# Keys laid out without padding in the attention of a hybrid kernel: two heads to 32 rows

## The chip, the cores and the metric

The kernel runs on one core of a Trainium2 chip. The metric is the device time in microseconds of one execution; with several runs, their median. TensorE (PE in the profile) multiplies matrices and transposes, VectorE (DVE) and ScalarE (ACT) work elementwise and take results out of PSUM, GpSimd (POOL) does small work, SyncE (SP) issues the DMAs.

## The reference, cut to what matters

One layer of a hybrid model runs over x of 4 x 1024 x 256, float32: a state-space block with a sequential scan over time, a mixture of 8 experts, an attention block with an MLP, and the same mixture again. The change touches the attention:

```
q, k, v = (einsum('bsd,dhm->bshm', x, w) for w in (wq, wk, wv))     # 16 heads of 16
phi_q, phi_k = relu(q) + 0.001, relu(k) + 0.001
kv  = cumsum(einsum('bshm,bshd->bshmd', phi_k, v), axis=1)
num = einsum('bshm,bshmd->bshd', phi_q, kv)
den = einsum('bshm,bshm->bsh', phi_q, cumsum(phi_k, axis=1))
attn_out = einsum('bshm,hmd->bsd', num / den[..., None], wo)
```

It is causal linear attention: within a chunk of 64 positions it is computed by scores and a mask, and what lies before the chunk comes in through running sums of phi_k v^T.

## The kernel before

A first part (`front_part`) normalises x, projects it, convolves, and writes the operands of the scan to DRAM; meanwhile SyncE loads the weights of the second part (L265). The second part (`main_part`) goes through the 1024 positions in 16 chunks of 64 positions by 4 batches, 256 tokens each (`TOK`), as two tiles of 128. Its loop is a software pipeline by hand: step i runs the scan of chunk i, the middle of chunk i-1 (gating, first mixture, attention) and the late part of chunk i-2 (MLP, second mixture). `step(1, 0, None)` has no late part and `step(None, 15, 14)` has no scan; so the attention runs 16 times, 14 of them in passes with all three parts.

Every engine's order is written out by hand, and engines meet only at semaphores.

- *Scan, VectorE.* 32 pairs of time steps to a chunk. One pair (`scan_pair`) is four multiplications (L1390) and four saturating additions (L1400), each on half the columns; a pair depends on the one before. After every fourth pair a small cblk product (L1375) follows.
- *Scan, TensorE.* `scan(1)` issues the inputs of the next pair, n+1 (`scan_inputs`, L974), which wait on `stepped` until VectorE has finished pair n-1, since they overwrite its bank; every fourth time the outputs of eight steps follow (`scan_output`, L989).
- *Attention, TensorE.* `features(w, j, made)` projects half of the key or query columns into bank `NB[j]`: 4 matmuls, each of which appears as two instructions in the trace (L1132). Values: L1290, into bank TB. `turn_k(tile)` (L1138) transposes the keys of one tile into TB, and ScalarE copies them to `ktok` (`copy_k`, L888). `scores` (L1149) has 128 small matmuls with 32 rows each; `from_states` (L1159), `from_chunk` (L1169) and `new_states` (L1180) follow.
- *Attention, VectorE.* `feature` (L1497) takes relu and adds epsilon from the bank into `kT` or `qT`, once for each half; `mask` (L1504) multiplies the scores.
- *Second mixture, beside it.* `late_first(e)` (L1055) and `late_second(e)` (L1068) are the layers of expert e of chunk i-2, `relu` (L879) lies between them on ScalarE, and `add_late(e)` (L1487) adds the result on VectorE. The scores wait for the fifth of these sums (`acc_done[1]`, `TILES * 5`), since they write its bank.

A head has 16 features, but the matmuls of the scores take rows in blocks of 32. So in the kernel before, wq and wk are padded: every head has 32 columns, of which the last 16 are zero, and 16 heads fill 4 groups of 128 rows (`GROUPS`), in q and in k.

## Time and profile before

| | |
|---|---|
| median of 3 runs | 2313.54 us (2308.51 to 2318.12) |
| the profiled execution | 2318.22 us, its span 2316.4 us |
| mean granted TensorE clock | 0.923 of full |
| TensorE (PE) busy | 1998.9 us, 86%, 18400 instructions |
| VectorE (DVE) busy | 1715.8 us, 74%, 6417 instructions |
| ScalarE (ACT) busy | 516.6 us, 22% |
| GpSimd (POOL) busy | 260.9 us, 11% |

A row of the timeline gives the start, the time from the first to the last end of the instructions that it merges, the engine, the line of the kernel, what is written and read, and the count; the bracket has the engine's idle time before it and who ended it. PE is the matmul itself and PEld the load of its weights; the ends of matmuls are modelled, and they are pipelined, so rows can overlap. In the chain that ended last, each piece is the time that the step added to the chain. Granted clock 1.00 is TensorE at 2.4 GHz and 0.50 at 1.2 GHz; a value between is a mean over a stretch.

### The profile page before, as it was taken

The page shows a single profiled execution, that of the slowest core. Times are in us where ns is not written, and L with a number is a line of the kernel's source. Part 1 is how long each engine was busy: PE and PEld are TensorE (multiplying, and loading weights), DVE is VectorE, ACT ScalarE, POOL GpSimd, SP SyncE. Part 2 cuts the span into 40 slices and gives each one's busy share as a digit, 9 for nine tenths or more (in the row PEclk, how much of TensorE's full clock was granted, in tenths as well). Part 3 has the DMA queues.
Part 4 walks back from the last instruction along what each step waited for, and adds up shares of the span by engine and source line. Part 5 has one row for each costly group of instructions (what it writes and reads, how often), then busy time and mean ns, then how long its engine had stood idle before and what let it go on. Part 6 is the DMA issues. An engine that isn't in the chain of part 4 may idle for free.

```text
span 2316.4 us, 59053 instructions
## 1 busy us (share of the span) xinstructions
PE 1998.9 (86%) x18400; PEld 1666.0 (72%) x18400; DVE 1715.8 (74%) x6417; ACT 516.6 (22%) x1078; POOL 260.9 (11%) x337
## 2 busy tenths in 40 slices
PE   7855788989898988989898989889898989899897
PEld 4432566878787877868787778778687877688786
DVE  4539777878787888778787878887887878787542
ACT  3330112122222222121212222221222122221221
POOL 0012002010101110010101110010101011100110
PEclk9865788999999999989998989999999999998998
DMA  7741100000000001000100101010001001010000
GB/s 254 222 119 31 30 12 22 14 25 12 19 23 12 25 12 30 12 26 14 27 12 15 26 11 26 12 30 12 25 13 29 12 12 30 11 27 7 6 2 10
DMA packets 100872, 73.51 MB, mean 32 GB/s; under 512 B 64488, under 2 KB 94448, under 8 KB 99568
## 3 DMA queue, kind: packets, MB, share of 16 engines
q1 hardware_dynamic: 100592, 69.91, 10.7%
q8 instruction: 160, 2.62, 0.5%
q14 instruction: 120, 0.98, 0.1%
HBM read 46.26 MB, written 23.59 MB: 30 GB/s over the span
## 4 chain that ended last, share of the span: by engine, by line
PE 54%; DVE 19%; issue 9%; SPq 7%; POOL 1%; DMA 1%; DVEq 1%; ACT 1%; POOLq 0%
PE bank L1068 17%; PE bank L1055 12%; DVE decayed_state L1390 6%; PE bank L1132 5%; DVE state L1400 4%; PE bank L974 4%; PE bank L989 3%; PE bank L1169 3%; PE bank L1010 2%; SPq L706 2%; SPq L724 1%; SPq L715 1%; PE bank L1202 1%; SPq L723 1%; SPq L722 1%
## 5 line engine op out<-in xcount | busy, mean ns | idle before, releaser
L1390 DVE TENSOR_TENSOR decayed_state<-state,decay 128x128 f32<-128x128 f32 x2048 | 567.7, 318 | 12.5 <-issue 8.7
L1400 DVE CUSTOM_DVE_ANT_0 state<-decayed_state,bank 128x128 f32<-128x128 f32 x2048 | 501.2, 285 | 61.5 <-PE bank L974 29.8
L1068 PE MATMUL bank<-f_w_sb,hs_whole 128*128 128x256 f32 x2048 | 510.1, 393 | 4.1 <-ACT hs_whole L879 4.1
L1068 PEld LDWEIGHTS bank<-f_w_sb,hs_whole 128*128 128x128 f32 x2048 | 382.5, 196 | 72.2 <-ACT hs_whole L879 21.7
L879 ACT ACTIVATE hs_whole<-bank,f_b_sb 128x256 f32<-128x256 f32 x512 | 214.7, 470 | 938.7 <-PE bank L1055 938.7
L974 PE MATMUL bank<-xrows,brows 128*128 128x256 f32 x1024 | 258.2, 345 | 87.1 <-DVE state L1400 53.4
L974 PEld LDWEIGHTS bank<-xrows,brows 128*128 128x128 f32 x1024 | 180.2, 212 | 130.4 <-issue 68.1
L1487 DVE SCALAR_TENSOR_TENSOR x<-bank,comb,x 128x256 f32<-128x256 f32 x256 | 111.8, 478 | 131.4 <-PE bank L1068 130.9
L989 PE MATMUL bank<-state,cblk 128*32 128x256 f32 x2048 | 156.4, 428 | 54.7 <-DVE state L1400 49.3
L1487 DVE SCALAR_TENSOR_TENSOR res<-bank,comb,res 128x256 f32<-128x256 f32 x256 | 112.1, 479 | 122.5 <-PE bank L1068 121.1
L801 POOL TENSOR_TENSOR m_ve<-m_mv,m_eps 128x2 f32<-128x2 f32 x96 | 19.2, 200 | 1539.8 <-DVE m_mv L1424 1539.8
L1055 PE MATMUL bank<-late_fT_parts,f_w_hi 128*128 128x256 f32 x1024 | 184.9, 304 | 0.0
L1055 PE MATMUL bank<-fT_parts,f_w_hi 128*128 128x256 f32 x1024 | 176.3, 299 | 0.0
L1055 PEld LDWEIGHTS bank<-late_fT_parts,f_w_hi 128*128 128x128 f32 x1024 | 148.7, 194 | 6.3 <-issue 0.7
L1055 PEld LDWEIGHTS bank<-fT_parts,f_w_hi 128*128 128x128 f32 x1024 | 144.6, 197 | 6.7 <-issue 5.3
L989 PEld LDWEIGHTS bank<-state,cblk 128*32 128x32 f32 x2048 | 57.4, 117 | 102.0 <-DVE state L1400 52.1
L1068 PE MATMUL bank<-m_w_sb,hs_whole 128*128 128x256 f32 x512 | 120.7, 379 | 0.0
L1068 PEld LDWEIGHTS bank<-m_w_sb,hs_whole 128*128 128x128 f32 x512 | 92.4, 189 | 10.1
L895 ACT ACTIVATE hs_whole<-bank,m_b_sb 128x256 f32<-128x256 f32 x128 | 53.6, 470 | 193.6 <-PE bank L1055 193.6
L1055 PE MATMUL bank<-late_fT_parts,m_w_hi 128*128 128x256 f32 x512 | 92.8, 308 | 0.0
L1055 PE MATMUL bank<-fT_parts,f_w_lo 128*128 128x256 f32 x512 | 84.0, 287 | 0.0
L1055 PE MATMUL bank<-late_fT_parts,f_w_lo 128*128 128x256 f32 x512 | 83.5, 286 | 0.0
(148 smaller groups left out, 2550.9 us busy)
## 6 DMA issues: line engine op xcount, KB each, us to landing
xrows<-xs_dram SPq DMA_DIRECT2D x512, 32.0 KB
brows<-bs_dram SPq DMA_DIRECT2D x1024, 2.0 KB
xt<-in_x SPq DMA_DIRECT2D x4, 1024.0 KB, 7.9
xn_dram<-xn SPq DMA_DIRECT2D x4, 1024.0 KB, 5.3
z_dram<-zT SPq DMA_DIRECT2D x4, 1024.0 KB, 4.1
f_w_sb<-in_f_w SPq DMA_DIRECT2D x2, 2048.0 KB
xs_dram<-xhi SPq DMA_DIRECT2D x4, 1024.0 KB, 4.6
xs_dram<-xlo SPq DMA_DIRECT2D x4, 1024.0 KB, 7.5
```

What stands on the lines that cost most here:

```text
L706: sp.dma_start(xrows[32 * q + 2 * B * j:32 * q + 2 * B * (j + 1), half % 2].bitcast(f32), g["xs_dram"][:, :, bass.ds(t0 + q * USTEPS, USTE ...
L879: act.activation(hs_whole[:, e % 2, m], hidden_bank(c, f, e)[:, m * TOK:(m + 1) * TOK], ACT.Relu, bias=g["f_b1"][:, e, m:m + 1]).then_inc( ...
L895: act.activation(hs_whole[:, j % 2, m], HB[j % 2][:, m * TOK:(m + 1) * TOK], ACT.Gelu_apprx_tanh, bias=g["m_b1"][:, 2 * j + m:2 * j + m + ...
L974: last = pe.matmul(U[n % 2][:, j * D:(j + 1) * D], brows[:, q * USTEPS + tq].rearrange("r b n -> r (b n)"), xrows[:, half % 2, tq, :], sta ...
L989: last = pe.matmul(Y[YCOLS * j:YCOLS * (j + 1), tile * D:(tile + 1) * D], cblk[:, slot * YCOLS:(slot + 1) * YCOLS], state[:, s % RING, :], ...
L1055: last = pe.matmul(dst(tile), *((w_, d_) if stationary == "w" else (d_, w_)), start=first and stationary != "more", stop=(n == len(PRODUCT ...
L1068: last = pe.matmul(bank_[:, tile * D:(tile + 1) * D], hs_whole[:, slot, m, tile * P:(tile + 1) * P], w(m), start=(m == 0 and tile == 0 and ...
L1132: last = pe.matmul(NB[j][:, gr % 2 * TOK:(gr % 2 + 1) * TOK], w[:, k, gr * P:(gr + 1) * P], fT[:, k, :], start=(k == 0), stop=(k == KD - 1))
L1169: last = pe.matmul(NB[tile][part, hd * HV:(hd + 1) * HV], ss[part, hh, tile * GROUPS + gr, :], vv[part, tile, hd, :], start=False, stop=(h ...
L1390: dve.tensor_tensor(decayed_state[:, part], state[:, (s - 1) % RING, part], decay[:, part], ALU.mult).then_inc(decayed.sem, 1)
L1400: dve._custom_dve(add_sat, out=state[:, s % RING, part], in0=decayed_state[:, part], in1=U[n % 2][:, s % 2 * D + h * HALF:s % 2 * D + (h + ...
L1487: dve.scalar_tensor_tensor(out=dst[:, tile], in0=out_bank(c, f, e)[:, tile * D:(tile + 1) * D], scalar=comb[:, f, tile, e:e + 1], in1=dst[ ...
```

## The change

The keys lose their padding: `KGROUPS = D // P` = 2 groups of 128 rows, in which a block of 32 rows holds two heads. The queries keep 4 groups; each head's 16 features stand at their place within the pair's block, and the rows of the other head hold zeros (from zero columns in wq and a zero in `feature_eps`, which has two columns now). So the product over 32 rows gives the scores of one head. The heads are renumbered by reordering the columns of wv and the rows of wo on the host. kT, ktok and the weights wk are half as large.

In `scores` and `new_states` the index of the key group becomes `gr % KGROUPS`. In the order of the engines: one key projection, one `feature` for k, one `turn_k` for both tiles and one `copy_k` remain; the wait for three experts' sums moves from before the second key projection to before the second query projection.

```diff
-    feature_eps = np.where(p % PADH < DH, KERNEL_EPS, 0.0).astype(np.float32)[:, None]
+    feature_eps = np.where(p[:, None] % PADH // DH == np.arange(PADH // DH)[None, :], KERNEL_EPS, 0.0).astype(np.float32)
...
-            def copy_k(c, tile):
-                act.wait_ge(k_tposed.sem, k_tposed.after(c, tile + 1))
-                act.activation(ktok[:, tile], TB[:], ACT.Copy).then_inc(k_copied.sem, 1)
+            def copy_k(c):
+                act.wait_ge(k_tposed.sem, k_tposed.after(c, 1))
+                act.activation(ktok[:].rearrange("p i k -> p (i k)"), TB[:], ACT.Copy).then_inc(k_copied.sem, 1)
...
-                def turn_k(tile):
-                    for gr in range(GROUPS):
-                        last = pe.transpose(TB[:, gr * P:(gr + 1) * P], kT[:, gr, tile * P:(tile + 1) * P], ident[:])
+                def turn_k():
+                    for tile in range(TILES):
+                        for gr in range(KGROUPS):
+                            at = (tile * KGROUPS + gr) * P
+                            last = pe.transpose(TB[:, at:at + P], kT[:, gr, tile * P:(tile + 1) * P], ident[:])
                     last.then_inc(k_tposed.sem, 1)
...
                 features(g["wk"], 0, k_made)
                 scan(1)
-                if late is not None:
-                    pe.wait_ge(acc_done[1].sem, acc_done[1].after(late, TILES * 3))
-                features(g["wk"], 1, k_made)
...
                 features(g["wq"], 0, q_made)
                 scan(1)
-                pe.wait_ge(kT_done.sem, kT_done.after(c, 2))
+                if late is not None:
+                    pe.wait_ge(acc_done[1].sem, acc_done[1].after(late, TILES * 3))
                 features(g["wq"], 1, q_made)
                 late_first(4)
                 pe.wait_ge(v_copied.sem, v_copied.after(c, TILES))
-                turn_k(0)
+                turn_k()
                 scan(1)
                 late_second(4)
+                scan(1)
+                pe.wait_ge(qT_done.sem, qT_done.after(c, 2))
                 pe.wait_ge(k_copied.sem, k_copied.after(c, 1))
-                turn_k(1)
-                scan(1)
-                pe.wait_ge(qT_done.sem, qT_done.after(c, 2))
-                pe.wait_ge(k_copied.sem, k_copied.after(c, TILES))
...
-                feature(0, k_made, kT, kT_done)
-                scan(1)
-                feature(1, k_made, kT, kT_done)
+                feature(0, k_made, kT, kT_done, lambda j: KERNEL_EPS)
+                scan(1)
                 add_late(3)
                 scan(1)
-                feature(0, q_made, qT, qT_done)
-                scan(1)
-                feature(1, q_made, qT, qT_done)
+                feature(0, q_made, qT, qT_done, lambda j: g["feature_eps"][:, j:j + 1])
+                scan(1)
+                feature(1, q_made, qT, qT_done, lambda j: g["feature_eps"][:, j:j + 1])
...
+    order = [H // KGROUPS * a + PADH // DH * slot + half for half in range(PADH // DH) for a in range(KGROUPS) for slot in range(GH)]
...
-        full = np.zeros((D, H, PADH), w.dtype)
-        full[:, :, :DH] = w
+        full = np.zeros((D, PADH // DH, H * DH // PADH, PADH // DH, DH), w.dtype)
+        for half in range(PADH // DH):
+            full[:, half, :, half] = w[:, half::PADH // DH]
```

## Rows read from the trace of the kernel before

**Rows 1.** The chain that ended last, on the page: share of the span by engine.
```profile
PE 54%; DVE 19%; issue 9%; SPq 7%; POOL 1%; DMA 1%; DVEq 1%; ACT 1%; POOLq 0%
```

**Rows 2.** Timeline of one pass: start us, us, engine, line, tiles, [idle before, releaser].
```profile
1079.01 0.59 PE L974 MATMUL bank<-xrows,brows 128*128 128x256 f32 x2
...
1079.40 0.75 DVE L1497 TENSOR_SCALAR kT<-bank,feature_eps_sb 128x512 f32<-128x512 f32 x1 [1.16 <-PE bank L1132]
1079.43 1.89 PE L1132 MATMUL bank<-turn,wk_sb 128*128 128x256 f32 x8
...
1081.40 0.49 DVE L1400 CUSTOM_DVE_ANT_0 state<-decayed_state,bank 128x128 f32<-128x128 f32 x2
...
1082.70 0.58 PE L974 MATMUL bank<-xrows,brows 128*128 128x256 f32 x2
...
1086.24 0.75 DVE L1497 TENSOR_SCALAR qT<-bank,feature_eps_sb 128x512 f32<-128x512 f32 x1 [1.03 <-PE bank L1132]
...
1092.61 0.88 DVE L1487 SCALAR_TENSOR_TENSOR x<-bank,comb,x 128x256 f32<-128x256 f32 x2 [1.47 <-PE bank L1068]
...
1092.96 0.60 ACT L888 ACTIVATE ktok<-bank 128x512 f32<-128x512 f32 x1 [2.04 <-PE bank L1138]
...
1093.79 1.59 PE L1149 MATMUL bank<-qT,kT 32*64 32x64 f32 x128 [0.63 <-ACT ktok L888]
...
1095.42 1.29 DVE L1504 TENSOR_TENSOR ss<-bank,causal_sb 128x512 f32<-128x512 f32 x2
```

**Rows 3.** Timeline of VectorE, feature maps (L1497) of other passes.
```profile
441.43 0.75 DVE L1497 TENSOR_SCALAR kT<-bank,feature_eps_sb 128x512 f32<-128x512 f32 x1 [1.14 <-PE bank L1132]
...
949.43 0.75 DVE L1497 TENSOR_SCALAR kT<-bank,feature_eps_sb 128x512 f32<-128x512 f32 x1 [1.16 <-PE bank L1132]
...
1205.43 0.75 DVE L1497 TENSOR_SCALAR kT<-bank,feature_eps_sb 128x512 f32<-128x512 f32 x1 [1.16 <-PE bank L1132]
...
2101.96 0.75 DVE L1497 TENSOR_SCALAR kT<-bank,feature_eps_sb 128x512 f32<-128x512 f32 x1 [1.16 <-PE bank L1132]
...
2108.81 0.75 DVE L1497 TENSOR_SCALAR qT<-bank,feature_eps_sb 128x512 f32<-128x512 f32 x1 [1.03 <-PE bank L1132]
```

**Rows 4.** Stretches: us, busy of PE, PEld, DVE, ACT, POOL; clock; DMA share; GB/s.
```profile
1079.00:1083.00 4.00, 4.00 (x21) 3.56 (x20) 3.57 (x13) 0.00 (x0) 0.00 (x0) 1.00 0.01 1
...
1095.00:1099.00 4.00, 3.20 (x64) 2.34 (x54) 3.94 (x15) 0.84 (x2) 0.00 (x0) 1.00 0.08 22
...
1115.00:1119.00 4.00, 1.52 (x21) 0.74 (x19) 3.94 (x14) 3.58 (x7) 2.14 (x3) 1.00 0.01 1
1119.00:1123.00 4.00, 2.73 (x10) 2.31 (x11) 2.93 (x11) 2.17 (x4) 0.80 (x1) 0.72 0.01 3
```

**Rows 5.** The chain that ended last, in order of time: start us, us, what.
```profile
1079.60 1.73 PE bank L1132 x8
...
1092.49 0.45 PE bank L1138 x4
```

**Rows 6.** Timeline of the same pass, just before rows 2.
```profile
1074.86 0.49 DVE L1400 CUSTOM_DVE_ANT_0 state<-decayed_state,bank 128x128 f32<-128x128 f32 x2
...
1075.26 0.88 DVE L1487 SCALAR_TENSOR_TENSOR x<-bank,comb,x 128x256 f32<-128x256 f32 x2
...
1075.40 0.50 PE L974 MATMUL bank<-xrows,brows 128*128 128x256 f32 x2 [1.05 <-DVE state L1400]
...
1075.74 1.89 PE L1068 MATMUL bank<-f_w_sb,hs_whole 128*128 128x256 f32 x8
```

**Rows 7.** Loading: the issue of the key weights, one stretch, and the third load's wait.
```profile
wk_sb<-in_wk SPq DMA_DIRECT2D x1, 512.0 KB
...
48.00:56.00 8.00, 6.87 (x46) 5.01 (x44) 2.93 (x8) 3.96 (x10) 0.00 (x0) 0.99 1.04 416
...
63.18 2.71 DVE L290 BATCH_NORM_STATS2 stats<-xt 128x6 f32<-128x256 f32 x8 [4.05 <-DMA xt<-in_x]
```

**Rows 8.** The chain in the first pass: start us, us, what.
```profile
312.86 2.94 PE bank L1132 x8
```

More of the change, by code:

```diff
@@ L38 @@
 GH = H // GROUPS
+KGROUPS = D // P
 HV = DH + 1
@@ L934, in step @@
                     relu(late, 1, 4)
[L935 to L936 removed]
+                copy_k(c)
                 if late is not None:
@@ L1148, in scores @@
                                     head = slice(PADH * hh, PADH * (hh + 1))
-                                    last = pe.matmul(SB[hh][CT * bb:CT * (bb + 1), at:at + CT], kT[head, gr, tok], qT[head, gr, tok],
+                                    last = pe.matmul(SB[hh][CT * bb:CT * (bb + 1), at:at + CT], kT[head, gr % KGROUPS, tok], qT[head, gr, tok],
                                                      start=True, stop=True, tile_position=(PADH * hh, CT * bb))
@@ L1178, in new_states @@
                             for hh in range(GH):
-                                first = gr * P + PADH * hh
+                                first = gr % KGROUPS * P + PADH * hh
                                 last = pe.matmul(TB[PADH * hh:PADH * (hh + 1), at:at + HV], ktok[part, tile, first:first + PADH],
@@ L1660, in lay_out @@
         "mlp_b2": row(a["attn_b_b2"]),
-        "wq": padded(a["attn_b_wq"]), "wk": padded(a["attn_b_wk"]),
-        "wv": blocks(a["attn_b_wv"].reshape(D, D)), "wo": blocks(a["attn_b_wo"].reshape(D, D)),
+        "wq": padded(a["attn_b_wq"]), "wk": blocks(a["attn_b_wk"].reshape(D, D)),
+        "wv": blocks(a["attn_b_wv"].reshape(D, H, DH)[:, order].reshape(D, D)),
+        "wo": blocks(a["attn_b_wo"].reshape(H, DH, D)[order].reshape(D, D)),
         "m_w1": blocks(a["attn_b_w1"]), "m_b1": per_partition(a["attn_b_b1"]), "m_w2": blocks(a["attn_b_w2"]),
```

24 lines of the change are left out of this document (11 added, 13 removed).

## The prediction

> **What bounds the kernel now.** I read the busy shares first (table above): TensorE 86%, VectorE 74%. The chain that ended last lies on TensorE for 54% and on VectorE for 19% [rows 1], so the lead changes hands. A share is an average over stages; the question is who waits for whom in the stage that the change touches. So I read the timeline of one loop pass, from the key projection to the masks [rows 2]. There TensorE runs through keys, a scan input (L974), keys again, values, a scan input and output and queries, with no idle time before any of them. VectorE follows with kT, a scan pair, kT, an expert sum and a scan pair, and waits for TensorE twice, for 1.16 us before the first kT and 1.03 us before the first qT. So TensorE leads this stretch. The reader should see how short the lead is: VectorE's scan pair behind the first kT ends at 1081.40 + 0.49 = 1081.89, and the scan input on TensorE that needs this pair starts at 1082.70. There is 0.81 us between them. From 1092.61 VectorE leads: the expert sum (L1487) ends at 1093.49, then come a scan pair and the masks, the first at 1095.42.
>
> The stage is the same in all 14 passes that have a scan and both neighbours: in each, the first qT starts 6.84 or 6.85 us after the first kT (this one and the last of them stand in rows 2 and 3). The pass as a whole is not. From kT to kT it takes 129.97 us in one case and 126.03 us in the next [rows 2, 3], and 127.7 us on average over 13 (441.43 to 2101.96) [rows 3]. With the same work in each, the difference is the clock: the rest of the pass holds stretches at the lower level [rows 4].
>
> **The change part by part.**
> *Second key projection, removed on TensorE.* Eight instructions, 1.73 us in the chain that ended last [rows 5]. With it gone, the values and then the next scan input move up by 1.73, to 1082.70 - 1.73 = 1080.97. But that scan input waits for the pair that VectorE ends at 1081.89, and this pair cannot move: it stands behind the first kT, which starts when the first half of the keys is done, and that is unchanged. So TensorE stops for about 0.9 us. A stop of just this kind stands earlier in the stage: VectorE ends a pair at 1074.86 + 0.49 = 1075.35, and L974 starts at 1075.40, 0.05 later [rows 6]. So it would start at 1081.94, a gain of 0.76. After a stop the next matmul follows L974 after 0.34 (1075.74 - 1075.40) [rows 6]; one that did not wait takes 0.42 (1079.43 - 1079.01) [rows 2]. That makes 0.84 at most. I take 0.8 per pass. This term, and not the 1.73, is the heart of the forecast.
>
> *Second kT, removed on VectorE.* 0.74 us of the engine, between 1081.9 and 1082.7. It moves the expert sum and the next scan pair up by as much. The first qT waits for TensorE (1.03 us idle before it [rows 2]), so what arrives there is TensorE's 0.8: VectorE's own 0.75 keeps pace and adds nothing. But without it the 0.8 would eat this reserve.
>
> *One turn of keys instead of two.* Four transposes (0.45 us in the chain [rows 5]) and one ScalarE copy of 0.60 us go. The scores waited until 1093.79 for the copy, which ended at 1092.96 + 0.60 = 1093.56; but they also wait for the expert sum of the other chunk, which ended at 1092.61 + 0.88 = 1093.49 [rows 2]. So the sum is late next, 0.07 us behind. The scores gain 0.1 to 0.25, and even that goes no further, because the first mask is set by VectorE (sum, scan pair, mask) and the scores end at 1093.79 + 1.59 = 1095.38, just before it. Worth: 0. The single turn that stays reads kT, which is ready long before, and waits for vv, as the first turn did. Its ScalarE copy stands where the first one stood, behind the same ReLU.
>
> *Moved wait.* The wait for three experts' sums stood before the second half of the keys and now stands before the second half of the queries. Behind it on TensorE are that projection, the first layer of expert 4, the turn and a scan input. The third sum ends at 1075.26 + 0.88 = 1076.14 [rows 6], 10 us before, so it costs nothing. VectorE's next sum (expert 3) moves with no new wait, since its product is there at 1075.74 + 1.89 = 1077.63 [rows 6].
>
> *Other edits.* The constant as an immediate for k and as one of two columns for q have the same shape and count, so 0. The scores and new_states keep their count and shapes (zeros in place of padding are multiplied as padding was), so 0, with -0.1 to +0.1 us per pass as bounds. Rows of kv_sum that held zeros now hold products with the neighbour head, met by zeros of the query: no time.
>
> *First and last pass.* The first has scans too, in the same order, and only no expert sum; I take it as a 15th pass of 0.8. The last has no scan: its 16 key instructions run in one piece, and nothing holds TensorE back. So 1.73 arrive there, and the scores, with no scan pair between the sum and the mask, pass on their 0.1 to 0.25 as well: 1.9.
>
> *Loading.* The key weights are 256 KB instead of 512. They are loaded while the DMA engines are full, at 416 GB/s, and VectorE then waits 4.05 us for the third load of x [rows 7]: 0.26 MB / 416 GB/s = 0.6 us. Bounds 0 and 0.6; I take 0.5, since x is issued behind them.
>
> **Sum.** 15 x 0.8 + 1.9 + 0.5 = 14.4 us. Against the profiled execution (2318.2 us) that gives 2303.8. That execution lies 4.7 us above the median of the three runs, so the median should be 2313.5 - 14.4 = 2299 us.
>
> **The clock as the unknown.** Removing dense matmuls and adding a stop of 0.9 us lowers the busy share of one stretch: 1079 to 1083 is busy for 4.00 of 4.00 us at granted clock 1.00 (2.4 GHz) and would be for about 3.1. The stretch 1095 to 1099, busy for 3.20, stands at 1.00 too. Behind a stretch of 1.52 the mean falls to 0.72, part of it at 1.2 GHz [rows 4]. So I cost the stop's effect on the clock at nothing.
> The Trainium skill (TensorE: Matmul & The Clock Gate, "A second HAM failure mode: psum-queue depth-cycling") says that an engine that idles briefly between groups of matmuls, often enough, swings between its two clock levels. By that rule the forecast would turn into the second rival; by the trace, where a stop of 1.05 us stands 6 us earlier [rows 6] and the clock stays full, it holds.
> The other effect is larger. Each pass gets 0.8 us shorter, so it falls elsewhere against the stretches at the lower level. Passes took from 126.0 to 130.0 us, 127.7 on average. If all 14 became short, the total would fall by another 14 x 1.7 = 24 us; if all became long, it would rise by 14 x 2.3 = 32. Neither is likely at once; a third of each, 8 less to 11 more, is what I allow for.
>
> **Rivals.**
> 1. *TensorE is the only bound.* Then 1.73 + 0.45 and the 0.63 us that TensorE idles before the scores [rows 2] arrive in each pass: 2.8 x 16 = 45 us, 2268. For it: TensorE's 54% of the chain. Against it: the 0.81 us of room [rows 2]. A milder form, 1.73 in each pass, gives 28 us: 2286. Chance 0.07 together, most of it on the milder one.
> 2. *The stop lowers the clock (slower).* Place: the two query projections behind the new stop. Eight such matmuls took 2.94 us at the lower level in the first pass [rows 8], against 1.73: 1.2 more. Both at the lower level cost 2.4 us per pass and 0.8 is gained, so it decides once it happens in every third pass. In all: 14 x (2.4 - 0.8) = 22 us slower, less the 3 of first pass, last pass and loading: 2333. Chance 0.05.
> 3. *The shorter pass meets more stretches at the lower level.* The 0.8 arrives, but 4 to 11 us go again: 2303 to 2310. Chance 0.25.
> 4. *It meets fewer of them*, by 7 to 14 us: 2285 to 2292. Chance 0.15.
> 5. *The change brings nothing*, because the scan pair holds TensorE to the old time: 2313. Against it: the 0.81 us of room. Chance 0.03.
> The forecast itself, 2292 to 2303, has 0.45.
>
> **How the numbers follow.** The range covers the forecast, most of 3 and 4 and the milder half of 1, and leaves out 2 and 5: 2286 to 2309. The bounds of the small costs (0.1 us per pass, 1.4 in all) lie inside it. A measurement of this kernel can tell about 0.5% from no change, and 0.5% below is 2302.0. Below it lie nearly all of the forecast, rival 1 and rival 4: 0.65. Within 0.5%: rival 3, rival 5 and the rest of the forecast: 0.30. Slower: 0.05.
>
> **What would show it.** Right: a new idle time of 0.8 to 1.0 us per pass before L974 behind the values, ended by VectorE's state; from the first kT to the first qT 6.0 to 6.1 us, not 6.84; the scores held by the sum (L1487), no longer by the ScalarE copy; passes of 126.9 us on average; in the last pass no new stop. Wrong: 5.1 us from kT to qT (rival 1), or a granted clock below 1.00 between kT and the masks (rival 2). A total off by more than 6 us with 6.0 to 6.1 us in place means rival 3 or 4.

## The result: 19 us slower, and the profile after

The changed kernel takes 2332.50 us (median of 7 runs, 2326.86 to 2339.04), the kernel before beside it 2313.54 us (median of 7, 2308.51 to 2321.66). The ratio is 1.0078, with a 95% interval of 1.0054 to 1.0102. The forecast was 2299 us. The profiled execution of after took 2332.50 us; its span is 2330.6 us against 2316.4 before, so the two profiles differ by 14.2 us. Its mean granted clock is 0.910 (0.923 before).

Busy time on the page of after: PE, DVE and ACT each did less work than before, and the end came later. The second line, the chain that ended last, answers to [rows 1].

```profile
PE 1989.3 (85%) x18208; PEld 1652.5 (71%) x18208; DVE 1709.7 (73%) x6401; ACT 506.9 (22%) x1062; POOL 260.8 (11%) x337
...
PE 52%; DVE 20%; issue 10%; SPq 7%; DVEq 1%; DMA 1%; POOL 1%; ACT 1%; POOLq 0%
```

So I read the stage first. The timeline of one pass of after, the counterpart of [rows 2], up to the first part of `from_chunk` (L1171) and the second layer of expert 5 (L1068):

```profile
1086.87 0.69 DVE L1495 TENSOR_SCALAR kT<-bank 128x512 f32<-128x512 f32 x1 [1.15 <-PE bank L1132]
...
1089.36 0.50 PE L974 MATMUL bank<-xrows,brows 128*128 128x256 f32 x2 [0.57 <-DVE state L1398]
...
1092.83 0.75 DVE L1495 TENSOR_SCALAR qT<-bank,feature_eps_sb 128x512 f32<-128x512 f32 x1 [0.76 <-PE bank L1132]
...
1099.22 0.87 DVE L1485 SCALAR_TENSOR_TENSOR x<-bank,comb,x 128x256 f32<-128x256 f32 x2 [1.48 <-PE bank L1068]
...
1100.15 1.59 PE L1151 MATMUL bank<-qT,kT 32*64 32x64 f32 x128 [0.82 <-DVE x L1485]
...
1101.92 1.28 DVE L1502 TENSOR_TENSOR ss<-bank,causal_sb 128x512 f32<-128x512 f32 x2
...
1103.99 0.49 DVE L1398 CUSTOM_DVE_ANT_0 state<-decayed_state,bank 128x128 f32<-128x128 f32 x2 [0.39 <-PE bank L974]
...
1105.22 1.28 DVE L1502 TENSOR_TENSOR ss<-bank,causal_sb 128x512 f32<-128x512 f32 x2
...
1106.04 1.17 PE L1161 MATMUL bank<-kv,qT 128*64 128x68 f32 x32 [1.44 <-DVE ss L1502]
...
1107.13 3.08 PE L1171 MATMUL bank<-vv,ss 64*64 64x17 f32 x64
...
1110.14 3.78 PE L1068 MATMUL bank<-f_w_sb,hs_whole 128*128 128x256 f32 x8
...
1116.39 0.63 PEld L1182 LDWEIGHTS bank<-vv,ktok 64*32 64x32 f32 x64
```

The same place of the kernel before, in the pass of [rows 2]: second masks, from_states, from_chunk, expert 5, new_states.

```profile
1098.37 1.28 DVE L1504 TENSOR_TENSOR ss<-bank,causal_sb 128x512 f32<-128x512 f32 x2
...
1099.19 1.17 PE L1159 MATMUL bank<-kv,qT 128*64 128x68 f32 x32 [0.99 <-DVE ss L1504]
...
1100.29 2.04 PE L1169 MATMUL bank<-vv,ss 64*64 64x17 f32 x64
...
1102.26 1.99 PE L1068 MATMUL bank<-f_w_sb,hs_whole 128*128 128x256 f32 x8
...
1106.39 0.73 PE L1180 MATMUL bank<-vv,ktok 64*32 64x17 f32 x64
```

Up to from_states everything is as forecast, and earlier than before. Then the same 64 matmuls take 3.08 us instead of 2.04, and the same eight 3.78 instead of 1.99. From from_states to new_states it takes 1116.39 - 1106.04 = 10.35 us; before it took 7.20. That is 3.15 us more, for no added instruction. The windows tell why. Columns as in [rows 4]. The kernel before:

```profile
1096.40:1100.40 4.00, 3.01 (x59) 2.16 (x59) 3.93 (x15) 0.84 (x2) 0.00 (x0) 1.00 0.16 43
1100.40:1104.40 4.00, 4.00 (x74) 3.65 (x74) 1.02 (x6) 0.00 (x0) 0.00 (x0) 1.00 0.11 30
```

The kernel after, at the same distance from the first kT (17 to 21, 21 to 25 and 25 to 29 us), and then four short windows around the two ends of the stretch:

```profile
1103.87:1107.87 4.00, 2.56 (x72) 1.93 (x66) 3.84 (x15) 0.37 (x2) 0.00 (x0) 0.99 0.22 67
1107.87:1111.87 4.00, 4.00 (x50) 3.68 (x47) 0.38 (x2) 0.00 (x0) 0.00 (x0) 0.50 0.04 7
1111.87:1115.87 4.00, 4.00 (x57) 3.30 (x56) 0.88 (x2) 0.00 (x0) 0.00 (x0) 0.66 0.00 0
...
1107.00:1107.80 0.80, 0.80 (x31) 0.73 (x27) 0.80 (x5) 0.00 (x0) 0.00 (x0) 1.00 0.24 72
1107.80:1108.60 0.80, 0.80 (x22) 0.80 (x20) 0.45 (x3) 0.00 (x0) 0.00 (x0) 0.50 0.17 46
1113.80:1114.60 0.80, 0.80 (x9) 0.57 (x9) 0.55 (x2) 0.00 (x0) 0.00 (x0) 0.50 0.00 0
1114.60:1115.40 0.80, 0.80 (x32) 0.80 (x30) 0.32 (x1) 0.00 (x0) 0.00 (x0) 0.98 0.00 0
```

From 1107.8 to 1114.6 the granted clock is 0.50 (1.2 GHz), while TensorE is busy all the time. VectorE has almost nothing to do there (0.38 of 4 us): TensorE leads, so each microsecond counts. Ahead of it stand the scores, three short groups, and an idle time of 1.44 us in which TensorE waits for the masks. I call this *the low stretch behind the masks*. It stands in 11 of the 14 passes of after, starting 20.8 to 21.1 us behind the first kT. I count a low stretch to it when it begins within 3 us of the start of from_states; in the kernel before there is 1 such pass of 14. All counts and pass lengths below come from one profiled execution of each kernel.

The first kT of the first two passes and of the last one, which answer to [rows 3]:

```profile
441.86 0.69 DVE L1495 TENSOR_SCALAR kT<-bank 128x512 f32<-128x512 f32 x1 [1.14 <-PE bank L1132]
...
571.57 0.69 DVE L1495 TENSOR_SCALAR kT<-bank 128x512 f32<-128x512 f32 x1 [1.16 <-PE bank L1132]
...
2123.15 0.69 DVE L1495 TENSOR_SCALAR kT<-bank 128x512 f32<-128x512 f32 x1 [1.15 <-PE bank L1132]
```

A pass takes (2123.15 - 441.86) / 13 = 129.33 us, against 127.73 before [rows 3]. That splits in two:

| per pass, mean of 13 | before | after | difference x 13 |
|---|---|---|---|
| kT to new_states | 26.99 | 29.04 (2 x 26.38, 11 x 29.52) | +26.6 |
| new_states to the next kT | 100.74 | 100.29 | -5.8 |
| kT to kT | 127.73 | 129.33 | +20.8 |

The start (first kT, 441.86 against 441.43) adds 0.4; what follows the last of these kT takes 2330.6 - 2123.15 = 207.4 us against 214.4, mainly since the one low stretch behind the masks of the kernel before stands there, 13.7 us long. 20.8 + 0.4 - 7.0 = 14.2: the whole difference between the two profiles. The slow part is one stage, and within it one cause: 11 x 3.15 = 34.7 us lost to the clock, 13 x 0.62 = 8.1 us saved, which makes the 26.6. Passes as long as these also occur without that stretch: four of the 13 before take 129.4 to 130.0 us, with other low stretches further on (in the pass from 1205.43, at 27.95, 41.6, 51.8 and 82.6 us behind kT). So the stretch accounts for this profile, but it is not the only way to a long pass.

### The profile page after: what moved, and what is told of

Read it like the earlier page. It is cut to its first block, busy times and chain, and to the rows that moved or that the text cites. A ratio compares the mean times of both kernels' runs of the same rounds, so it can differ in the third digit from the quotient of the medians.

```text
span 2330.6 us, 58595 instructions
## 1 busy us (share of the span) xinstructions
PE 1989.3 (85%) x18208; PEld 1652.5 (71%) x18208; DVE 1709.7 (73%) x6401; ACT 506.9 (22%) x1062; POOL 260.8 (11%) x337
## 4 chain that ended last, share of the span: by engine, by line
PE 52%; DVE 20%; issue 10%; SPq 7%; DVEq 1%; DMA 1%; POOL 1%; ACT 1%; POOLq 0%
PE bank L1068 18%; PE bank L1055 11%; DVE decayed_state L1388 6%; DVE state L1398 5%; PE bank L1132 4%; PE bank L974 4%; PE bank L1171 3%; PE bank L989 3%; PE bank L1010 2%; DVE x L1485 2%; SPq L707 1%; SPq L725 1%; PE bank L1204 1%; SPq L716 1%; PE bank L1331 1%
## 5 line engine op out<-in xcount | busy, mean ns | idle before, releaser
L1068 PE MATMUL bank<-f_w_sb,hs_whole 128*128 128x256 f32 x2048 | 524.7, 402 | 4.2 <-ACT hs_whole L880 4.2
L1068 PEld LDWEIGHTS bank<-f_w_sb,hs_whole 128*128 128x128 f32 x2048 | 389.7, 200 | 74.5 <-ACT hs_whole L880 22.1
L974 PE MATMUL bank<-xrows,brows 128*128 128x256 f32 x1024 | 263.8, 351 | 98.1 <-DVE state L1398 62.9
L974 PEld LDWEIGHTS bank<-xrows,brows 128*128 128x128 f32 x1024 | 184.0, 216 | 149.1 <-DVE state L1398 70.3
L1485 DVE SCALAR_TENSOR_TENSOR x<-bank,comb,x 128x256 f32<-128x256 f32 x256 | 112.0, 479 | 155.5 <-PE bank L1068 155.0
L1485 DVE SCALAR_TENSOR_TENSOR res<-bank,comb,res 128x256 f32<-128x256 f32 x256 | 112.1, 480 | 117.6 <-PE bank L1068 116.1
L1068 PE MATMUL bank<-m_w_sb,hs_whole 128*128 128x256 f32 x512 | 120.7, 379 | 0.0
L1068 PEld LDWEIGHTS bank<-m_w_sb,hs_whole 128*128 128x128 f32 x512 | 92.4, 189 | 10.1
L1055 PEld LDWEIGHTS bank<-late_fT_parts,m_w_hi 128*128 128x128 f32 x512 | 82.0, 219 | 1.9 <-issue 0.8
```

Of the source, the lines that this page charges most:

```text
L974: last = pe.matmul(U[n % 2][:, j * D:(j + 1) * D], brows[:, q * USTEPS + tq].rearrange("r b n -> r (b n)"), xrows[:, half % 2, tq, :], sta ...
L1055: last = pe.matmul(dst(tile), *((w_, d_) if stationary == "w" else (d_, w_)), start=first and stationary != "more", stop=(n == len(PRODUCT ...
L1068: last = pe.matmul(bank_[:, tile * D:(tile + 1) * D], hs_whole[:, slot, m, tile * P:(tile + 1) * P], w(m), start=(m == 0 and tile == 0 and ...
L1485: dve.scalar_tensor_tensor(out=dst[:, tile], in0=out_bank(c, f, e)[:, tile * D:(tile + 1) * D], scalar=comb[:, f, tile, e:e + 1], in1=dst[ ...
```

## The experiments

Each ran with the kernel before beside it on its chip, and the ratio is to those runs. The rounds ran on three chips, where the median of before was 2315.16 us (e1 to e4), 2309.71 (e5 to e8), 2312.35 (e9 to e12) and 2308.48 (e13 to e16); between rounds the ratios compare better than the times. "Pass" is the mean from kT to kT in the one profile, "low" the number of its 14 passes with the low stretch behind the masks. The profiled execution is not always a typical one: that of e9 was the fastest of its ten (2294.07), that of e13 the fastest of its seven (2287.25), that of e11 the slowest of its eleven (2318.28).

| kernel | median us | ratio to before (95%) | pass | low |
|---|---|---|---|---|
| before | 2313.54 | 1 | 127.73 | 1 |
| after | 2332.50 | 1.0078 (1.0054 to 1.0102) | 129.33 | 11 |
| e1 dense second | 2333.10 | 1.0079 (1.0053 to 1.0106) | 128.62 | 4 |
| e2 late pair | 2331.25 | 1.0062 (1.0032 to 1.0093) | 129.18 | 3 |
| e3 delay elsewhere | 2336.10 | 1.0087 (1.0062 to 1.0113) | 129.81 | 5 |
| e4 before, longer | 2342.10 | 1.0115 (1.0062 to 1.0168) | 129.29 | 0 |
| e5 fill masks | 2306.71 | 0.9982 (0.9949 to 1.0014) | 127.31 | 0 |
| e6 before, fill masks | 2315.12 | 1.0031 (1.0012 to 1.0050) | 127.40 | 0 |
| e7 fill all | 2332.57 | 1.0102 (1.0057 to 1.0147) | 129.39 | 0 |
| e8 before, fill all | 2332.56 | 1.0102 (1.0059 to 1.0144) | 128.92 | 0 |
| e9 before, shorter | 2303.25 | 0.9957 (0.9924 to 0.9990) | 126.47 | 0 |
| e10 delay 1.6 | 2335.68 | 1.0085 (1.0058 to 1.0112) | 129.57 | 7 |
| e11 fill stage | 2307.88 | 0.9983 (0.9960 to 1.0006) | 127.72 | 0 |
| e12 before again | 2314.96 (one run) | | 127.49 | 1 |
| e13 real fill | 2294.98 | 0.9934 (0.9906 to 0.9961) | 126.08 | 0 |
| e14 before, real fill | 2317.96 | 1.0033 (1.0014 to 1.0053) | 127.52 | 0 |
| e15 real fill, both gaps | 2287.47 | 0.9890 (0.9850 to 0.9931) | 126.43 | 0 |
| e16 before, both gaps | 2318.46 | 1.0031 (1.0012 to 1.0051) | 128.90 | 0 |

**First round: is it the removed dense work, the new stop, or neither?** e1 puts the second key projection back into the changed kernel, as work whose result nobody reads:

```diff
                 scan(1)
+                if late is not None:
+                    pe.wait_ge(acc_done[1].sem, acc_done[1].after(late, TILES * 3))
+                for gr in range(2):
+                    for k in range(KD):
+                        pe.matmul(NB[1][:, gr * TOK:(gr + 1) * TOK], g["wk"][:, k, gr * P:(gr + 1) * P],
+                                  fT[:, k, :], start=(k == 0), stop=(k == KD - 1))
```

> The changed kernel, with the second key projection issued again on TensorE as work whose result nobody reads (eight matmul instructions into the second bank, at their old place, behind the wait for three experts' sums). The second kT and the second turn stay out. Theory A (activity): the granted clock falls behind the masks because the dense matmuls are gone and idle time stands in their place; with them back no stretch at the lower level starts behind the masks, the first qT follows the first kT after about 6.8 us, and the time is that of the kernel before, 2308 to 2322. Theory B (position): the clock falls there because the pass is shorter and lies elsewhere; the pass is as long as before, so the same, 2308 to 2322. Theory C: it is the missing second turn and its copy that matter: 2326 or more, with the low stretch behind the masks still there.

Measured: 2333.10 us. The first qT starts 6.85 us behind kT again (1093.96 and 1100.81 in the pass below), the stop is gone, and the time stays that of after. So neither the eight removed matmuls nor the stop costs the 19 us; theories A and B fell. What theory C forecast came: 2326 or more, with the stretch still there (4 passes). It blamed the missing second turn and its copy, and no run put these back alone, so it stands. It fits that the scores, freed from that copy, start 14.15 us behind kT in e1 (14.40 before), while the masks still come late and the wait for them stays 1.45 us. Its profile shows something better than its time: two passes, at the same distance from kT, the first without the low stretch and the second with it.

```profile
1110.96:1114.96 4.00, 2.53 (x53) 1.75 (x52) 3.58 (x14) 0.84 (x2) 0.00 (x0) 1.00 0.21 49
1114.96:1118.96 4.00, 4.00 (x80) 3.69 (x76) 1.23 (x6) 0.00 (x0) 0.00 (x0) 1.00 0.10 24
...
1239.63:1243.63 4.00, 2.56 (x54) 1.77 (x52) 3.58 (x14) 0.84 (x2) 0.00 (x0) 1.00 0.20 49
1243.63:1247.63 4.00, 4.00 (x75) 3.71 (x70) 1.24 (x6) 0.00 (x0) 0.00 (x0) 0.62 0.08 24
```

TensorE did the same in both, 2.53 and 2.56 us of 4. Afterwards the clock is 1.00 in one and 0.62 in the other. So the gap before the masks is not enough; something that differs from pass to pass, such as when the pass comes by, decides as well. Passes with the stretch take 130.5 to 131.0 us, the others 126.4 to 128.7. Against the profile of before, the 13 passes of e1 are 11.6 us longer: some 15.7 more to new_states (four stretches of 3.15 us, and 0.24 us in each pass: 27.23 behind kT, 26.99 in before) and 4 less in the rest. The first kT comes 7.5 us later (448.94 against 441.43), and what follows the last one is 4.3 shorter; together 14.8. So half of what e1 is slower in its profile arises ahead of the attention's regular passes.

e2 lets VectorE read the keys twice (`feature(0, k_made, spare, ...)` behind the first), so that the scan pair is nearly as late as before and the stop longer (the first query projection then waits for both; that part of the edit isn't shown). e3 adds 0.8 us per pass on VectorE at another place, before the layernorm ahead of the MLP (LN2), as two operations (the second part of the diff); e4 adds 2.5 us there to the kernel before, with `range(6)`.

```diff
                 feature(0, k_made, kT, kT_done, lambda j: KERNEL_EPS)
+                feature(0, k_made, spare, kT_done, lambda j: KERNEL_EPS)
...
+                for n in range(2):
+                    dve.tensor_scalar(spare[:, n], a_t[:, n % TILES], 1.0, None, ALU.mult)
```

> The changed kernel, and VectorE takes relu and epsilon of the keys a second time, into a buffer that nobody reads, directly behind the first and before the scan pair (0.75 us). TensorE then waits about 1.5 us for the pair instead of 0.6, so the stage has the timing of the kernel before (first kT to first qT 6.7 to 6.8 us) but not its dense work. Theory A (activity): the low stretch behind the masks stays in most passes, and the time is 2330 to 2350. Theory B (position): timing as before, so positions as before, 2308 to 2322, and no low stretch behind the masks.

> The changed kernel, with two VectorE instructions of 0.4 us (a copy of a_t that nobody reads) before the last layernorm of the attention block, where TensorE waits for VectorE anyway. The attention stage is as in the changed kernel, the pass is 0.8 us longer elsewhere, as long as before. Theory A (activity in the stage): the low stretch behind the masks stays, and the time is that of the changed kernel or up to 12 us more, 2328 to 2350. Theory B (position): the pass falls as it did before; no low stretch behind the masks in most passes, 2308 to 2322.

> The kernel before, with six VectorE instructions of 0.4 us (copies of a_t that nobody reads) at the place of the third experiment: the same work in the attention stage, but a pass longer by 2.5 us, so it falls elsewhere against the stretches at the lower level. Both theories: at least 14 x 2.5 = 35 us more, 2348. Theory A (activity): with the second projection in place no low stretch starts right behind the masks, 2340 to 2352. Theory B (position): some or all passes show the low stretch right behind the masks, with dense work before it unchanged, 2355 to 2385.

Measured: 2331.25, 2336.10 and 2342.10. In e2 the first qT comes 6.55 us behind kT instead of 5.96, the wait for the masks is 1.1 us, 3 passes have the low stretch, and the time doesn't rise. In e3, 14 x 0.8 = 11 us of added work cost 3.6 us. In e4, 14 x 2.5 = 35 us cost 27, with no low stretch behind the masks. All three times lie in the ranges of theory A, which e1 had already refuted (and in e2 it wanted the stretch in most passes); theory B's ranges failed in all three. The number of those stretches changes from kernel to kernel (3, 5 and 0), but the time does not follow it alone: e2 and e3 have 3 and 5 and are as slow as after with 11. No sum of instructions gives these times either; they leave room for a theory in which the place of the pass against the low stretches decides, which the next rounds test. Two passes of e3 show a long pass without the stretch behind the masks: their starts, 129.69 us apart, and the windows 17 to 21 and 21 to 25 us behind the first of them.

```profile
1610.43 0.69 DVE L1496 TENSOR_SCALAR kT<-bank 128x512 f32<-128x512 f32 x1 [1.16 <-PE bank L1133]
...
1740.12 0.69 DVE L1496 TENSOR_SCALAR kT<-bank 128x512 f32<-128x512 f32 x1 [1.16 <-PE bank L1133]
...
1627.43:1631.43 4.00, 2.53 (x74) 1.90 (x63) 3.84 (x15) 0.34 (x1) 0.00 (x0) 1.00 0.26 66
1631.43:1635.43 4.00, 4.00 (x76) 3.63 (x74) 1.02 (x4) 0.00 (x0) 0.00 (x0) 1.00 0.04 8
```

**Second round: close the gap.** e5 puts three matmuls without use into the wait for the masks of the changed kernel; e6 two into that of the kernel before, where the wait is shorter.

```diff
+                def busy(bank_, times):
+                    for n in range(times):
+                        pe.matmul(bank_[:, 0:TOK], g["wv"][:, n % KD, 0:P], g["wv"][:, n % KD, 0:TOK], start=True, stop=True)
...
                 late_first(5)
                 scan(1)
+                if late is not None:
+                    pe.wait_ge(relued[1].sem, relued[1].after(late, F // P * 6))
+                busy(HB[0], 3)
                 pe.wait_ge(masked.sem, masked.after(c, 3))
```

> The changed kernel, with three dead float32 matmuls (six instructions, about 1.3 us, weights times weights into the bank of expert 5's hidden layer once ScalarE has read it) where TensorE waits 1.44 us for the masks. Nothing that is needed gets later. Theory B' (position and a gap: the clock falls behind the masks where a stretch that the chip judges ends 7.5 to 8.4 us after the first score, in every kernel so far, and the changed kernel's passes come back to that place): with the wait filled that place no longer lowers the clock; no low stretch starts 20 to 23 us after the first kT, and the time is 2285 to 2305. Theory A (missing dense work among the projections): the low stretch stays, 2325 to 2340.

> The kernel before, with two such dead matmuls (four instructions, 0.87 us) in its wait of 1.0 us for the masks. Theory B': it met that place in 1 of 14 passes only, so little is to be had, 2300 to 2318; other low stretches stay. If filling a wait helps any kernel alike, it gains as much as the changed one does, 30 us or so, 2280 to 2290.

Measured: e5 takes 2306.71 us, 26 us less than after (22 by the ratios), by adding work; it is level with before (the interval holds 1) and 2 us above what theory B' allowed. e6 takes 2315.12, 0.3% more than the before beside it. The timeline of e5 (kT, then the filled gap), and the same two windows as for after:

```profile
1073.63 0.69 DVE L1502 TENSOR_SCALAR kT<-bank 128x512 f32<-128x512 f32 x1 [1.15 <-PE bank L1132]
...
1091.27 1.56 PE L1145 MATMUL bank<-wv_sb 128*128 128x256 f32 x6
1092.81 1.17 PE L1165 MATMUL bank<-kv,qT 128*64 128x68 f32 x32
1093.91 2.04 PE L1175 MATMUL bank<-vv,ss 64*64 64x17 f32 x64
...
1090.63:1094.63 4.00, 4.00 (x79) 2.96 (x71) 3.84 (x15) 0.36 (x1) 0.00 (x0) 1.00 0.26 68
1094.63:1098.63 4.00, 4.00 (x76) 3.63 (x74) 1.02 (x4) 0.00 (x0) 0.00 (x0) 1.00 0.04 6
```

from_states starts 1092.81 - 1073.63 = 19.18 us behind kT, as in after (19.17): the dead matmuls delay nothing. What follows is at clock 1.00, in all 14 passes, and kT to new_states takes 26.37 us, not 29.04: 13 x 2.67 = 34.7 us come back. Of these 8.4 go again in the rest of the pass (127.31 - 26.37 = 100.94 against 100.29), which leaves 26. Closing the gap gives nothing in the kernel before, which had hardly a stretch there to lose.

e7 also fills the gap before the scores (1), the new stop (1) and, with six matmuls, the wait for LN2 ahead of the MLP; e8 does so in the kernel before. e11 is e7 without the six (the last part of the diff, shortened by the waits that stand between).

```diff
+                busy(HB[0], 1)
                 scan(1)
...
+                busy(HB[0], 1)
                 scores()
...
+                busy(HB[1], 6)
                 mlp_input(c)
```

> The changed kernel with dead matmuls in four waits of TensorE: three before the masks, one before the scores, one in the new stop behind the values, six before the turn for the MLP, where it waits 3.8 us for the layernorm. Expected: no low stretch behind the masks and fewer behind the layernorm; passes of 122 to 125 us and a time of 2255 to 2290. If the low stretches behind the layernorm come from elsewhere, 2285 to 2305 as in the fifth.

> The kernel before with dead matmuls in three waits: two before the masks, one before the scores, six before the turn for the MLP. It is the partner of the seventh: with the clock kept up in both, the change should show what the sum said for it, 14 us less (0.9 x 15 and the last pass), so this one 10 to 20 us above the seventh. If the gain of the changed stage is lost elsewhere too, the two lie within 5 us.

> The fifth experiment (dead matmuls in the wait for the masks), with one more before the scores and one in the new stop behind the values; the wait for the layernorm stays empty. If the place behind the masks was the whole loss, nothing is added: 2295 to 2312, like the fifth. If the fill before the layernorm was what cost the seventh its gain, this one is 20 us or more faster than the seventh; if the fills inside the stage cost it, it is slow too, 2325 or more.

Measured: 2332.57, 2332.56 and 2307.88. e11 equals e5, as its expectation said: with the gap before the masks closed, the stop and the gap before the scores are worth nothing more. e7 missed its own by over 40 us, and of e8's two cases the second came: the two lie within 5 us. The six matmuls ahead of the MLP are all that e7 has more than e11, and they cost it 25 us (27 by the ratios): its passes take 129.39 us, though the gap before the masks is closed, and in most of them a low stretch of 10.2 us stands 48 to 59 us behind kT. e8 is 17 us slower than e6; there a part comes from the matmul before the scores, which start 0.46 us later (14.86 behind kT, not 14.40). Filling is no good in itself; it can bring low stretches elsewhere.

**Third round: is a shorter pass dangerous by itself?** e9 leaves out of the kernel before the first half of the affine of LN2 (the mean isn't subtracted and the scale not applied), 0.8 us of VectorE per pass, the size of the saving of the change. e10 adds 1.6 us per pass to after, as e3 does but with `range(4)`. e12 is the kernel before once more.

```diff
-                    for tile in range(TILES):
+                    for tile in range(TILES if k != LN2 else 0):
```

> The kernel before, with the first half of the last layernorm's affine step left out on VectorE (mean and scale are not applied; two instructions, 0.8 us, where VectorE leads). The attention stage keeps all its work; the pass is 0.8 us shorter, as the change made it, but in another place. Theory B' (position): passes come to the place where a low stretch starts 7.5 to 8.4 us after the first score; it is seen in 4 or more of 14 passes, against 1 of 14 in the kernel before, and the time is 2305 to 2335 although work was taken out. Theory A (it needs the work missing from the stage): no more such passes than before, and 2296 to 2306.

> The changed kernel with four copies of 0.4 us on VectorE before the last layernorm, where the third experiment had two: a pass longer by 1.6 us. If the time simply adds up, 2332 + 15 x 1.6 = 2357. Theory B' (position): the pass length is set by where it falls, so up to all of the 24 us can be absorbed, 2325 to 2345, with fewer than 12 passes that show the low stretch behind the masks.

> The kernel before, unchanged: a second profile of it. In the first, 1 pass of 14 showed the low stretch behind the masks. If the changed kernel differs from it by that, again at most 2 of 14 do.

Measured: e9 takes 2303.25 us, 0.9957 of before (9 us for 11 saved), with no low stretch behind the masks. The expectation that a shorter pass would bring it, in 4 passes or more, was wrong. In its profile, the fastest of its ten runs, the first nine passes all take 126.1 to 126.4 us, so this kernel can hold a short pass. e10 costs 3 us where 22 were added, within what theory B' had said. e12 has one low stretch behind the masks, like the first profile of before. So as far as one profile tells, the shorter pass alone doesn't do it. The changed kernel differs from e9 in the gap: 1.44 us instead of 0.98, and at another distance from kT. Over all profiles the stretch goes with the gap: in 4 to 11 passes where it is 1.4 to 1.5 us (after, e1, e3, e10), in 3 where it is 1.1 (e2), in 0 or 1 where it is 1.0 (before, e4, e9, e12), in none where it is filled. That is an order over runs and not a test of its own.

**Fourth round: close the gap with real work.** Open by then: whether e5 and e11 escaped only because dead work gave their passes another length, and whether the saving of the change shows once the gap is closed. e13 and e14 move the first layer of expert 6, which stood behind new_states(0), before the wait for the masks, in after and in before: the same instructions in another order. e15 and e16 also move the second layer of expert 7 ahead of the waits for the MLP's input.

```diff
                 late_first(5)
                 scan(1)
+                late_first(6)
                 pe.wait_ge(masked.sem, masked.after(c, 3))
...
                 new_states(0).then_inc(kv_half.sem, 1)
-                late_first(6)
                 scan(1)
...
+                late_second(7)                # e15, e16
                 if late is not None:
                     pe.wait_ge(xr_done.sem, xr_done.after(c, 1))
                 pe.wait_ge(kv_added.sem, kv_added.after(c, 1))
                 mlp_input(c)
-                late_second(7)                # e15, e16
```

> The changed kernel, whole computation. The first layer of late expert 6 (TensorE work of about 0.9 us at the full clock) moves from behind the first new_states to before the wait for the masks, so that real work stands where the kernel with three dead matmuls had them. Theory B' (the low stretch behind the masks is the whole loss, and work in the gap takes it away): no low stretch begins within 3 us behind the masks in any of the 14 passes; passes of 126 us or less on average, 2282 to 2300 us. Rival D (only dead work, which adds to TensorE's work, takes it away, because it moves the pass to another length): low stretches behind the masks stay in at least 5 of 14 passes, and the time stays at 2320 to 2340. Rival F (the low stretches only move to another place): none behind the masks, but the sum of the low time stays, 2305 to 2325.

> The kernel before with the same move of the first layer of late expert 6. The whole computation. Theory B': the kernel before has hardly a low stretch behind the masks, so the move brings only the idle time that it fills, up to 1.0 us per pass: 2297 to 2312. With the changed kernel in the same order, the difference is the price of the change without its low stretch: B' expects the changed one to be 5 to 20 us faster. Rival F: no difference between the two, or the changed one slower again.

> As the changed kernel with late expert 6's first layer in the gap before the masks, and in addition the second layer of late expert 7 moved ahead of the waits for the MLP's input, where TensorE idles for some 3.7 us. The whole computation. Theory B': both gaps carry real work, the second brings up to 1.7 us per pass: 2255 to 2290, no low stretch behind the masks. Rival F: the time that the second move saves goes again in low stretches: 2280 to 2310.

> The kernel before with both moves (first layer of late expert 6 before the wait for the masks, second layer of late expert 7 ahead of the waits for the MLP's input). The whole computation. Theory B': 2270 to 2300, and 5 to 20 us slower than the changed kernel with both moves. Rival F: equal to it within 5 us or faster than it.

Measured: 2294.98 and 2317.96; 2287.47 and 2318.46. e13 and e15 came within theory B', e14 and e16 above it. In equal order the changed layout is 23 us faster than the old one, and with both moves 31 us (5 to 20 were expected of both); the highest run of either changed kernel (2299.59, 2289.85) lies below the lowest run of its partner (2312.00, 2312.66). The moves themselves cost the old layout 0.3% (e14 and e16 against the before beside them). Against that before in its own order, e13 is 14 us (0.7%) faster and e15 21 (1.1%). The two changed kernels in the new order beat both original ones. One pass of e13: kT, TensorE between the masks and from_chunk, and the two windows:

```profile
1068.23 0.69 DVE L1495 TENSOR_SCALAR kT<-bank 128x512 f32<-128x512 f32 x1 [1.15 <-PE bank L1132]
...
1085.84 0.74 PE L1055 MATMUL bank<-late_fT_parts,f_w_hi 128*128 128x256 f32 x4
1086.42 0.63 PE L1055 MATMUL bank<-late_fT_parts,f_w_lo 128*128 128x256 f32 x4
1086.88 0.64 PE L1055 MATMUL bank<-late_fT_parts,f_w_hi 128*128 128x256 f32 x4
1087.45 1.17 PE L1161 MATMUL bank<-kv,qT 128*64 128x68 f32 x32
1088.55 2.04 PE L1171 MATMUL bank<-vv,ss 64*64 64x17 f32 x64
...
1085.23:1089.23 4.00, 4.00 (x84) 3.31 (x72) 3.87 (x15) 1.16 (x3) 0.00 (x0) 1.00 0.22 61
1089.23:1093.23 4.00, 4.00 (x77) 3.62 (x74) 0.95 (x4) 0.00 (x0) 0.00 (x0) 1.00 0.05 12
```

from_states starts 1087.45 - 1068.23 = 19.22 us behind kT, against 19.17 in after: 12 matmul instructions went into the gap for 0.05 us. In e14 the same row and its kT are these:

```profile
1083.34 0.75 DVE L1497 TENSOR_SCALAR kT<-bank,feature_eps_sb 128x512 f32<-128x512 f32 x1 [1.16 <-PE bank L1132]
...
1103.70 1.17 PE L1159 MATMUL bank<-kv,qT 128*64 128x68 f32 x32
```

20.36 us, against 19.79 in before: the twelve instructions take 1.61 us (1085.84 to 1087.45 above), not the 0.9 that I had expected, its gap of 0.99 us is too short for them, and 0.57 us of the move stick out. That would be 8 us in 14 passes, of the 9.5 by which e14 lies above the before beside it. It isn't shown to be the reason, since the passes of its profile are no longer than those of before (127.52 and 127.73). e16 missed its own by 18 us, and its second move gained nothing: nine of its 13 passes take 129.4 to 130.1 us and carry 17.1 to 20.5 us of low stretches. e13 and e15 have none behind the masks, without any added work.

## Why the prediction was wrong, point by point

*The new stop, 0.8 per pass: right.* It stands in every pass before L974, ended by VectorE's state (0.57 us on the matmul, 0.97 on the weight load), and kT to qT is 5.96 us in each, 0.88 less (I took 0.8, and named 6.0 to 6.1). Some 0.05 of it is the constant, which I had put at nothing: with an immediate, the feature map of the keys takes 0.69 us, not 0.75, and the pair behind it ends that much sooner. That the stop costs the clock nothing held as well: the window from 1088.87 to 1092.87 is busy for 3.51 of 4.00 us, at clock 1.00.

*What holds the scores: right in kind.* They wait for the sum (L1485). They start 13.28 us behind kT, not 14.40: 1.12 earlier, of which I had 0.8 from the projection and up to 0.25 from the copy.

*What arrives behind them: sized wrongly.* I let the 0.8 pass through. The first masks come 15.05 us behind kT (16.02 before), the second 18.35 (18.97), because VectorE now waits 0.39 us for the scan input between them (the row at 1103.99), and from_states starts 0.62 earlier. So 0.5 of the 1.12 us didn't get through, and TensorE's wait for the masks grew from 0.99 to 1.44. The text said of this place only that VectorE sets the mask. It never asked what TensorE does while it waits, and that wait is where the loss begins.

*Last pass, 1.9: right.* From the first kT to the first qT it takes 3.46 us instead of 5.18 (1.72 less, with no stop), and the scores come 1.84 earlier, measured from kT.

*Loading, 0.5: too small, and lost again.* VectorE's wait for x moved from 63.18 to 61.83, 1.35 earlier. But the first kT comes at 317.59, not 315.84: the first 300 us hold low stretches too, and they fell differently.

*The clock: the step that failed.* "A third of each, 8 less to 11 more, is what I allow for." I had taken the places of the low stretches as chance, independent from pass to pass, so that most of it would even out; I allowed 11 us more and named 126.9 us for a pass. Measured are 129.33 us for a pass and 34.7 us lost at one place. Ten passes with the low stretch behind the masks follow one another (starts 827.34 to 1994.74), nine of them 129.6 to 129.9 us long, each with the stretch at the same place to 0.2 us; e9 and e12 repeat at 126.1 to 126.4 without it. So a pass seems to hand its place to the next, and the error isn't 14 small ones that even out, it is one, 11 times: 34.7 us lost and 8.1 saved up to new_states, 5.8 won back in the rest of the passes.

*The rivals.* Rival 2 gave the right time (2333) by luck, with the wrong mechanism: it put the lower clock at the query projections, behind the new stop, and there it stays at 1.00; I gave it 0.05. Rival 3, "meets more stretches", was the right kind and stopped at 11 us. What neither had is a gap that was already there, some 16 us behind the new stop, and lengthened by the saving itself. The Trainium skill (TensorE: Matmul & The Clock Gate, "A second HAM failure mode: psum-queue depth-cycling") describes short idle times between groups of matmuls as a cause of such swings. I had held a single row against it, a stop of 1.05 us after which the clock stayed; the trace of after agrees with the page some 16 us later, where the clock falls behind waits of 0.82 and 1.44 us and 3.15 us are lost in 11 passes. What decides in which pass it falls stays open: in e1 the same 2.5 us of work left the clock full in one pass and not in another.

*What is shown and what is not.* Shown: in the profile of after the loss is the low stretch behind the masks (times and windows), and work in the gap before it removes it, whether dead (e5, e11) or real (e13, e15): none in 56 passes. Shown: in an order that closes the gap the changed layout is 23 to 31 us faster than the old one. Of that, 1.14 us per pass stand in the stage (from_states 19.22 us behind kT against 20.36), some 16 us in 14 passes, and half of that (0.57) is what the move costs the old layout, whose gap is shorter; the rest wasn't traced to a place. Not shown: which part of the change lengthens the gap and brings the stretch. The shorter stage goes together with the missing second turn, and theory C of e1 has no test of its own. Not shown: why the passes of the changed kernel come back to that place and those of e9, shortened as much, don't. e3 and e10 move it by 0.8 and 1.6 us and find 5 and 7 such passes, so the answer isn't in the added time alone. Nor is it settled why e1, e2 and e3, with only 4, 3 and 5 of them, are no faster than after. In e3 most of the other passes are as long (129.5 to 129.7 us), with low stretches further on; the time at the lower clock doesn't tell either: 10.2 us per pass in e7, whose passes take 129.39, and 10.0 in e13, whose take 126.08.

## What to carry to other kernels

Before you cost a saving ahead of a wait, follow it to the next place where the engine idles on the path: the saving may arrive there as idle time, and if dense matmuls follow that are on the path, the clock can take back several times as much (here 0.45 us of added idle time came with a loss of 3.15 in 11 of 14 passes). In a loop, a clock effect needn't even out: one low stretch can stand at the same place in most passes (11 of 14 here, 3 to 7 in the variants), so allow for that sum as well. When a change that removes work comes out slower, read the granted clock by windows at one distance from a fixed instruction of each pass, and try to move independent real work into the gap before the low stretch (12 instructions moved here: from 0.8% above the kernel before to 0.7% below it).

## What was not expected of the hardware

- Work of 0.8 to 2.5 us added to each pass costs less than its sum (3.6 us for 11, 3.2 for 22, 27 for 35), and dead matmuls can make a kernel faster (e5, 26 us below after, though no faster than before).
- The lengths that repeat from pass to pass are 126.0 to 126.5 us (e9, e12, e13, e15) or 129.2 to 130.2 us (after, e3, e4, e7, e10, e16), in kernels whose work differs by up to 2.5 us per pass. In these kernels 9 to 12 of the 13 passes lie there (7 in e12); the kernel before has 4 passes in each of the two.
- The same 4 us of TensorE work (2.53 and 2.56 us busy, e1) is followed by clock 1.00 in one pass and 0.62 in another.
- The mean granted clock says little about the time: the profiled execution of after has 0.910 and takes 2332.5 us, that of e15 has 0.911 and takes 2289.9. In e15 most passes have low stretches at 28 to 31 and 41 to 55 us behind kT and still take 126.2 to 126.4 us. In one of the latter (below) TensorE is busy for 9.55 of 13.66 us and VectorE for 10.97, where behind the masks of after TensorE had no idle time and VectorE hardly any work. So what seems to count is whether TensorE leads where the clock is low.

```profile
1241.83:1255.49 13.66, 9.55 (x51) 7.99 (x51) 10.97 (x39) 4.12 (x8) 3.85 (x3) 0.50 0.09 22
```
